# Attention times values with the values stationary in four column groups, and a ScalarE regrouping in place of a VectorE transpose

## What is computed

```python
h = _layernorm(x, g1, b1)
q, k, v = h @ Wq + bq, h @ Wk + bk, h @ Wv + bv      # 16 heads, 4 key/value heads, 8 wide
q, k = _rope(q), _rope(k)
scores = einsum('bhqd,bhkd->bhqk', q, k) / sqrt(8)
valid = (col <= row) & (row - col < 32)               # a window of 32 keys
attn = softmax(where(valid, scores, -1e9))
out = einsum('bhqk,bhkd->bhqd', attn, v)
x = x + (out @ Wo + bo)
x = x + gelu(_layernorm(x, g2, b2) @ Wf1 + bf1) @ Wf2 + bf2
# experts: the two best of eight for each token, silu(x w1) * (x w3), then w2
```

## Time and profile before

| | |
|---|---|
| median of three runs | 522.35 us |
| profiled execution | 519.14 us |
| its span | 517.3 us |
| PE busy | 448.0 us (87%) |
| VectorE (DVE) busy | 382.3 us (74%) |
| ScalarE (ACT) busy | 249.6 us (48%) |
| GpSimd (POOL) busy | 225.0 us (43%) |

### The profile page before, as it was taken

One profiled execution on the slowest core, in us unless ns is written; L12 is line 12 of the kernel. 1 busy time (PEld: TensorE's weight loads), 2 busy tenths in 40 slices (PEclk: granted clock), 3 DMA queues, 4 the chain that ended last, 5 costly groups with the idle time before them and its releaser, 6 DMA issues.

```text
span 517.3 us, 11263 instructions
## 1 busy us (share of the span) xinstructions
PE 448.0 (87%) x3374; PEld 414.7 (80%) x3375; DVE 382.3 (74%) x1019; ACT 249.6 (48%) x532; POOL 225.0 (43%) x252
## 2 busy tenths in 40 slices
PE   3944976869999999999999999999999999997846
PEld 2834976869989898989898989998989778786533
DVE  6858773776877777777777787867878788577682
ACT  2592004545554555555546464555554564653302
POOL 3630012534555555555555555555544553033110
PEclk9975556998999999999999999999999999999788
DMA  7850022443444544444544343434340500001431
GB/s 221 223 184 0 1 89 80 134 133 103 139 149 123 158 119 151 126 149 120 153 128 154 118 156 116 151 118 155 120 121 2 164 2 0 2 1 61 123 101 41
DMA packets 33667, 56.77 MB, mean 110 GB/s; under 512 B 5967, under 2 KB 21203, under 8 KB 33505
## 3 DMA queue, kind: packets, MB, share of 16 engines
q1 hardware_dynamic: 28160, 47.22, 29.9%
q0 software_dynamic: 4608, 8.93, 5.8%
q10 hardware_dynamic: 864, 0.20, 0.2%
HBM read 47.94 MB, written 8.91 MB: 110 GB/s over the span
## 4 chain that ended last, share of the span: by engine, by line
PE 57%; issue 16%; ACT 14%; DVE 10%; POOL 2%; DVEq 1%; ACTq 0%; POOLq 0%
PE bank L1136 17%; PE bank L1149 11%; PE bank L1100 5%; PE bank L1163 5%; PE bank L1174 4%; PE bank L1099 4%; PE bank L1065 3%; PE bank L1078 3%; ACT qbd L894 3%; ACT act L919 3%; DVE inter L741 2%; ACT gT_sb L871 2%; ACT L918 2%; DVE x_sb L751 1%; ACT act L918 1%
## 5 line engine op out<-in xcount | busy, mean ns | idle before, releaser
L1136 PE MATMUL bank<-xsT,w_sb 128*128 128x128 f32 x1008 | 132.2, 284 | 13.0 <-DVE inter L741 10.2
L1136 PEld LDWEIGHTS bank<-xsT,w_sb 128*128 128x128 f32 x1008 | 120.9, 195 | 18.7 <-issue 17.8
L401 POOL DMA_INDIRECT scratch_ys<-ysb,pair x72 | 77.9, 1082 | 122.5 <-ACT ysb L925 112.1
L394 POOL DMA_INDIRECT xsb<-scratch_xn,token x72 | 73.5, 1021 | 71.2 <-DVE token L572 45.5
L1149 PE MATMUL bank<-w_sb,inter 128*128 x576 | 79.9, 282 | 4.5 <-issue 3.2
L1149 PEld LDWEIGHTS bank<-w_sb,inter 128*128 128x128 f32 x576 | 70.3, 192 | 8.0 <-issue 7.7
L925 ACT ACTIVATE ysb<-bank 128x128 f32<-128x128 f32 x72 | 19.8, 275 | 84.1 <-PE bank L1149 84.1
L1100 PE MATMUL bank<-dv,pO 128*128 128x36 f32 x256 | 49.8, 278 | 1.3 <-ACT h2T_sb L879 1.3
L739 DVE TENSOR_TENSOR inter<-bank,act 64x128 f32<-64x128 f32 x72 | 21.2, 294 | 37.4 <-ACT act L919 32.2
L888 ACT ACTIVATE kT<-bank 32x256 f32<-32x256 f32 x64 | 23.8, 372 | 38.9 <-issue 38.4
L1100 PEld LDWEIGHTS bank<-dv,pO 128*128 128x128 f32 x256 | 39.9, 196 | 2.7 <-issue 2.7
(11 more groups left out here) (147 smaller groups left out, 841.4 us busy)
## 6 DMA issues: line engine op xcount, KB each, us to landing
w_sb<-in_w SPq DMA_DIRECT2D x72, 448.0 KB
w_sb<-scratch_ys SPq DMA_DIRECT2D x8, 512.0 KB, 4.5
scratch_xn<-xn_sb SPq DMA_DIRECT2D x8, 256.0 KB, 3.7
w_sb<-in_w SPq DMA_DIRECT2D x1, 2048.0 KB, 9.2
out_dram<-x_sb SPq DMA_DIRECT2D x8, 256.0 KB, 3.6
xsb<-scratch_xn,token POOLq DMA_INDIRECT x72
scratch_ys<-ysb,pair POOLq DMA_INDIRECT x72
x_sb<-in_x SPq DMA_DIRECT2D x3, 256.0 KB, 4.0
```

Of the source, the lines that this page charges most:

```text
L394: nc.gpsimd.indirect_dma_start(xsb[:, j % 3, :], None, xn, bass.IndirectOffsetOnAxis(ap=token[:, j:j + 1], axis=0)).then_inc(slots_in[j % ...
L401: nc.gpsimd.indirect_dma_start(ys, bass.IndirectOffsetOnAxis(ap=pair[:, j:j + 1], axis=0), ysb[:, j % 3, :], None, bounds_check=2 * NTOK - ...
L1136: last = nc.tensor.matmul(to[:, c % EC * P:(c % EC + 1) * P], w13_sb[:, i % 3, c * P:(c + 1) * P], xsT[:, p, :], start=True, stop=True)
```

## The change

The two operands of `attend` change places. The values (vbd and dv, now 32 columns) are stationary, and the weights (pT and pO, 128 columns) move. The result of block n goes to the 32 partitions of column group n % 4 and to one of two ranges of 128 columns, so the features of a key/value head are on the partitions and the queries in the free dimension. Quarters 0 and 2 run eight matmuls each, pT with vbd and pO with dv for four blocks, block 0 included. Quarters 1 and 3 run four each, in which the mask of ones is stationary and pO moves and which give the row sums, each repeated over the partitions of its head, in another 256 columns of the bank. `norm` takes the reciprocal of all 256 columns on all partitions and multiplies; its transpose goes. In its place ScalarE copies `on` into outT, 16 copies a batch of 32 partitions by 64 elements, from the partitions of a block's group to those of a head group (`regroup`): four behind the first copy of own scores, four behind the key copies, eight behind take_h2T, all in the step after the norm. The columns of ones leave vbd and dv, and with them three VectorE copies and a GpSimd memset of the prologue.

```diff
-VW = NKV * HD + NKV
+VW = NKV * HD
...
-        rsum = sb("rsum", [P, NBLK, NKV])
+        rsum = sb("rsum", [P, T])
...
-            nc.gpsimd.memset(dv[:, :, 1:NBLK, NKV * HD:VW], 0.0)
...
-            nc.vector.tensor_copy(identb_sb, ident_sb)
-            nc.vector.tensor_copy(dv[:, :, 0, NKV * HD:VW],
-                                  bc(vmask_sb[:, NKV * HD:VW].rearrange("p (a c) -> p a c", a=1), [P, 2, NKV]))
-            for p in range(2):
-                last = nc.vector.tensor_copy(
-                    vbd[:, p, 1:NBLK + 1, NKV * HD:VW],
-                    bc(vmask_sb[:, NKV * HD:VW].rearrange("p (a c) -> p a c", a=1), [P, NBLK, NKV]))
-            last.then_inc(consts_set, 1)
+            nc.vector.tensor_copy(identb_sb, ident_sb).then_inc(consts_set, 1)
...
             def norm(b):
                 dve.wait_ge(pv_psum, b + 1)
-                pv = turn_bank[:, 0:NBLK * VW].rearrange("p (n c) -> p n c", c=VW)
-                nc.vector.reciprocal(rsum, pv[:, :, NKV * HD:VW]).then_inc(rsum_ready, 1)
+                nc.vector.reciprocal(rsum, turn_bank[:, T:2 * T]).then_inc(rsum_ready, 1)
                 dve.wait_ge(rsum_ready, b + 1)
-                nc.vector.tensor_tensor(
-                    on.rearrange("p (n h d) -> p n h d", h=NKV, d=HD),
-                    pv[:, :, 0:NKV * HD].rearrange("p n (h d) -> p n h d", d=HD),
-                    bc(rsum.rearrange("p n (h a) -> p n h a", a=1), [P, NBLK, NKV, HD]), ALU.mult).then_inc(pv_normed, 1)
-                dve.wait_ge(pv_normed, b + 1)
-                nc.vector.transpose(outT, on).then_inc(outT_ready, 1)
+                if some(b):
+                    dve.wait_ge(outT_ready, b)
+                nc.vector.tensor_tensor(on, turn_bank[:, 0:T], rsum, ALU.mult).then_inc(pv_normed, 1)
...
+            def regroup(b, g):
+
+                if g == 0:
+                    act.wait_ge(pv_normed, b + 1)
+                    if some(b):
+                        act.wait_ge(wo_psum, b)
+                for c in range(4):
+                    last = nc.scalar.activation(
+                        outT[g * 32:(g + 1) * 32, :].rearrange("p (a n q) -> p a n q", a=2, n=4)[:, :, c, :],
+                        on[c * 32:(c + 1) * 32, :].rearrange("p (a g q) -> p a g q", a=2, g=G)[:, :, g, :], ACT.Copy)
+                if g == G - 1:
+                    last.then_inc(outT_ready, 1)
...
                 if exists(k):
                     keep_own(k, 0)
+                if exists(k - 2):
+                    regroup(k - 2, 0)
...
                 if exists(k + 1):
                     take_keys(k + 1, 1 - p)
+                if exists(k - 2):
+                    regroup(k - 2, 1)
...
                 if exists(k - 3):
                     take_h2T(k - 3)
+                if exists(k - 2):
+                    regroup(k - 2, 2)
+                    regroup(k - 2, 3)
...
-                for n in range(quarter * NBLK // 4, (quarter + 1) * NBLK // 4):
-                    to = turn_bank[:, n * VW:(n + 1) * VW]
-                    if n > 0:
-                        nc.tensor.matmul(to, pT[:, n].rearrange("p g q -> p (g q)"), vbd[:, p, n, :], start=True, stop=False)
-                    last = nc.tensor.matmul(to, pO[:, n].rearrange("p g q -> p (g q)"), dv[:, p, n, :], start=(n == 0), stop=True)
+                a, total = quarter // 2, quarter % 2
+                for i in range(1 if total else 2):
+                    for c in range(4):
+                        n = 4 * a + c
+                        to = turn_bank[32 * c:32 * c + 32, total * T + a * P:total * T + (a + 1) * P]
+                        weights = (pO if i else pT)[:, n].rearrange("p g q -> p (g q)")
+                        values = vmask_sb if total else dv[:, p, n, :] if i else vbd[:, p, n, :]
+                        last = nc.tensor.matmul(to, values, weights, start=(i == 0), stop=(i == 1 or total == 1))
```

More of the change, by code:

```diff
@@ L53 @@
 QKV = (NH + 2 * NKV) * HD
-VW = NKV * HD + NKV
+VW = NKV * HD
+assert VW == WIN
 NO_PAIR = 1e6
@@ L645, in values @@
                 nc.vector.tensor_tensor(
-                    vbd[:, p, 1:NBLK + 1, 0:NKV * HD], vt.rearrange("p (n c) -> p n c", n=NBLK),
-                    bc(vmask_sb[:, 0:NKV * HD].rearrange("p (a c) -> p a c", a=1), [P, NBLK, NKV * HD]),
+                    vbd[:, p, 1:NBLK + 1, :], vt.rearrange("p (n c) -> p n c", n=NBLK),
+                    bc(vmask_sb.rearrange("p (a c) -> p a c", a=1), [P, NBLK, NKV * HD]),
                     ALU.mult).then_inc(vbd_ready, 1)
@@ L653, in value_steps @@
                     dve.wait_ge(pv_psum, b - 1)
-                nc.vector.tensor_tensor(dv[:, p, :, 0:NKV * HD], vbd[:, p, 1:NBLK + 1, 0:NKV * HD],
-                                        vbd[:, p, 0:NBLK, 0:NKV * HD], ALU.subtract).then_inc(dv_ready, 1)
+                nc.vector.tensor_tensor(dv[:, p], vbd[:, p, 1:NBLK + 1, :], vbd[:, p, 0:NBLK, :], ALU.subtract).then_inc(dv_ready, 1)
             def shift(b, h):
@@ L1292, in constants @@
     qmask = np.where((p // HD % NKV)[:, None] == np.arange(NKV), 1.0 / np.sqrt(f32(HD)), 0.0).astype(f32)
-    col = np.concatenate([np.repeat(np.arange(NKV), HD), np.arange(NKV)])
+    col = np.repeat(np.arange(NKV), HD)
     vmask = ((p // WIN)[:, None] == col).astype(f32)
```

## The result

The changed kernel takes 526.1 us, the median of seven runs (525.43 to 529.21), against 521.92 us for seven runs of the kernel before on the same chip: a ratio of the means of 1.010, interval 1.0072 to 1.0129. That is slower by 4.2 us in the medians, less than 2%, but with 1 outside the interval. The profiled execution took 525.43 us with a span of 523.4, 6.1 us more than the span before.

A forecast was written before the change was run, and what follows sets the result against it. PE was taken to bound both stages, with the silu-inter-tile chain close behind. Loop +6.0, tail +4.6 and prologue -0.3 gave +10.3 on 519.14, 529.4 us, raised to a 530.5 median; own range 524 to 537, overall 515 to 546.

The forecast's parts named there:

- The chain of tile 1: Expert loop: four copies between own scores and silu, in a chain without slack, delay PE's tile 2 by 0.92 us.
- Regroup 1 hides in the shift: Expert loop: the second four copies, before silu of tile 2, fall into the first 0.92 us delay and add nothing.
- Attention at 3.0 us a batch: PE's attention: 2.66 us of stream plus 0.34 for tile-shape changes, against 3.33 before, a gain of 0.33 us a batch.
- rival B: PE's attention: all four column groups stream side by side, 1.4 us a batch, total 513 to 516 us; chance 0.18.
- the lower bound of 1.33: PE's attention stream: 1.33 us a batch if all four column groups stream side by side; 2.66 was taken.
- rival D: Array empties at each tile-shape change (0.167 us, attention 4.0), or reciprocal near 2.8 us; 536 to 546 us; chance 0.12.
- Regroups 2 and 3 hidden with 0.5 us to spare: Expert loop: eight copies behind take_h2T let inter end at 314.8, before PE wants tile 5 at some 315.3.
- A step of the loop, +0.6: Each of ten loop steps with a regroup: 0.92 us of copies less 0.33 of attention, +6.0 us in all.
- The norm: VectorE's reciprocal grows to 1.75 us, yet ends just in time for PE's heads, by 0.1 us; costs nothing in the loop.
- The prologue: Before the loop: the three copies of mask columns go, -0.3 us.
- The tail: Behind the loop: copies 5.1 + 0.2, longer norm 0.95, attention gain -1.7 us, together +4.6 us.
- The sign: Slower rather than faster, chance 0.66; loop and tail cancel at an attention batch of about 2.2 us, faster below it.

The follow-up runs named there:

- the joined quarters: Changed kernel with all copies in ScalarE's idle places, plus attention quarters 0 and 1, and 2 and 3, run back to back: 498.01 us, ratio 0.975 to the kernel before.
- the short reciprocal: Changed kernel with the norm's reciprocal over 32 of its 256 columns and a constant in the rest: 521.54 us, ratio 1.0233 to the kernel before.
- the later run of after: The changed kernel run again unchanged, on a chip of the faster kind: 522.49 us, ratio 1.0226 to the kernel before.

## Why the prediction was right, and where it wasn't

The forecast was slower, 530.5 us, and the time is 526.1: the right side and within the forecast's own range of 524 to 537. The sum stood for the profiled execution, +10.3 us, which has 525.43 - 519.14 = +6.3. By its terms:

- **The chain of tile 1 (right).** 0.92 us for four copies and tile 2 at 4.57: measured 1.04 us for the four (253 ns each in the mean; 0.23 was foreseen) and 4.57. Four copies alone in the kernel before showed it apart from all else.
- **Regroup 1 hides in the shift (right in effect).** Tile 3 adds only 0.14. The first four moved early showed the cover: regroup 1 then costs what regroup 0 did.
- **Attention at 3.0 us a batch (mis-sized twice).** The two terms were 2.66 for the stream and 0.34 for changes of shape. Measured: 48 instructions at 0.030 are 1.44, and the rest of the 2.43 is 0.99 for eight changes, 0.12 each. All four groups ran side by side, as rival B had it, and the lower bound of 1.33 was the row to take. The gain is 3.33 - 2.43 = 0.90 us, not 0.33. The Trainium skill (TensorE: Matmul & The Clock Gate, part 3) has matmuls in distinct column groups run concurrently, and the trace agrees. The Trainium skill, TensorEngine Tiling (Array Packing), Key Properties, has a change of tiling mode drain TensorE; the gaps of 0.17 and 0.20 us beside the quarter shown agree with that, and a change costs 0.12 us, or 0.11 by the joined quarters, less than the 0.167 that rival D gave it.
- **Regroups 2 and 3 hidden with 0.5 us to spare (wrong).** The text said that this cover would be gone with an attention of 1.4 us; 2.43 was enough, with eight copies that took 2.11 us instead of 1.84. PE waits 0.59 us for tile 5, the distance stays at 4.51, and the first half of the 0.90 is lost there. The second half, 4.80 to 4.31, is kept: 0.49.
- **A step of the loop, +0.6 (right, as a sum of these).** 26.34 against 25.79 is +0.55: +0.92 and +0.14 in tiles 1 to 3, -0.49 behind tile 5. On the faster kind of chip it is +1.13, since the kernel before has no wait of 0.50 us for a late update there, into which the longer chain could fall. The forecast was made from the one trace and holds for that kind of chip.
- **The norm (right).** 1727 ns against 1.75 us, the end in time for heads, and the short reciprocal gained nothing.
- **The prologue (-0.3 foreseen, -1.3 between the two profiles).** Tile 0 of step 0 starts at 82.73 instead of 84.02. How much of that is the copies that went can't be told from two executions: it starts at 83.7 to 84.0 in the three traces with the old prologue and at 82.2 to 83.8 in the eleven with the new one, 0.9 apart in the mean. Behind that the granted clock, 0.50 (1.2 GHz) from 40 to 84 us, rises to 2.4 GHz (0.74 and 0.82 in the six us from 84 on, before and after, then 1.00); the next tile starts 4.79 us later before, 4.95 after, and 6.11 in the later run of after. That much moves between executions.
- **The tail (+4.6 foreseen, +2.0 measured).** The copies are the term that held: 5.3 us foreseen, and on the faster kind of chip the tail after is 121.8 - 116.3 = 5.5 us longer than without copies. What was mis-sized is the rest, attention and norm, foreseen at -0.75 (-1.7 + 0.95): there the tail without copies is 120.6 - 116.3 = 4.3 us shorter than before, mostly five batches of attention at 0.90 instead of 0.33. Steps 12, 13 and 14 grow by 1.05, 2.07 and 0.61, against 1.7 less 0.33 foreseen for each. The projection's copies of the last steps were taken as hidden, and aren't: PE waits there for outT, 2.79 us by the line below.

```profile
503.78 0.71 PE L1119 MATMUL bank<-wo_sb,outT 128*128 128x128 f32 x4 [2.79 <-ACT outT L897]
```

So the main error is one, the price of the attention. In the loop it nearly cancelled against the cover that the shorter attention no longer gave; that the step came out at +0.55 for +0.6 is in part luck. In the tail it did not cancel and is most of the 4 us between +10.3 and +6.3. The sign, too, was nearer than the chances said: the text had it turn under some 2.2 us a batch, and the measured 2.43 stands just above. What no term held is the answer's dependence on the chip: a ratio of 1.010 on one, 1.0226 on another.

## What to carry to other kernels

Ask of each instruction that is moved to an idle engine what stands behind it in that engine's order, not how busy the engine is: 256 copies of 253 ns cost 22 us in the change's places, mostly ahead of silu, and some 2 us in the gaps behind it. When a cover is counted on, work out by how much the change itself shortens it. And before taking one delay out of a chain, look for the next one that hides behind it: moving the first four copies gained nothing in the loop, because the next four took their place; moving all sixteen made the kernel 20 us faster.

## What was not expected of the hardware

- Float32 matmuls with 32 stationary columns in four column groups start every 0.030 us, 128 columns moving, whatever the order of the groups; each change between such a quarter and 128-column matmuls costs PE about 0.12 us, and joining two quarters brought the next tile 0.22 us nearer.
- Chips differ by 2% on one kernel (510 and 522 us for the kernel before), at a granted clock of 0.923 and 0.927. On the slower ones some of PE's semaphore updates come late, by 0.50 us in one line and up to 2.1, with nothing of the kind on the faster ones. A change can cost more than twice as much on one as on another.
- Four ScalarE copies alone, 1.05 us long, made a step 1.42 us longer: a delay can come out of a chain larger than it went in. Which meeting of engines adds the rest is open.
